# Transposes on two row halves, dt transposes behind slot 5, and a new order of the end, in a fused Mamba and feed-forward layer

## The reference, cut to what matters

```
# layer 1: a mixing of the tokens by condition, then a state space layer
h     = mixed tokens of x                       # [64, 32, 512]
proj  = h @ in_proj_w.T                         # gate 4096, x/B/C 6144, dt 64
xBC   = silu(causal conv of 4 taps over time of proj's x, B, C)
dt_p  = softplus(dt + dt_bias);  A = -exp(A_log)
state = state * exp(dt_p * A) + dt_p * x * B    # for each of 64 heads, 32 steps
y     = state . C + x * D
out   = (y * rsqrt(mean square of its group) * norm_weight * silu(gate)) @ out_proj_w.T
x     = x + out
# layer 2: grouped conv of 9 taps + context, then a dense layer with a selection
v     = conv(x) + c @ c_weight.T + bias
dots  = softmax(v @ centroids.T / 0.1);  hits = dots > 0.01
dense = v @ weight.T + bias
x     = x + where(any hit in this row & cluster of this column was hit, dense, 0)
```

## Time and profile before

| | us |
|---|---|
| median of 3 runs | 1626.84 (1625.94 to 1626.89) |
| the profiled execution's own time | 1627.06 |
| its span | 1625.3 |
| PE busy | 1604.8 (99%) |
| DVE busy | 1059.1 (65%) |
| ACT busy | 845.9 (52%) |
| POOL busy | 773.4 (48%) |

### The profile page before, as it was taken

How to read it: one execution, slowest core, us unless ns; L and a number is a source line. 1 busy time by engine, 2 the same in 40 slices (tenths; PEclk the granted TensorE clock), 3 DMA queues, 4 the chain that set the end, 5 groups by cost and what they waited for, 6 DMA issues and landing times. The chain is left out here.

```text
span 1625.3 us, 31516 instructions
## 1 busy us (share of the span) xinstructions
PE 1604.8 (99%) x12495; PEld 1299.1 (80%) x12495; DVE 1059.1 (65%) x1741; ACT 845.9 (52%) x1372; POOL 773.4 (48%) x731
## 2 busy tenths in 40 slices
PE   9999999999999999999999999999999999999997
PEld 6778888888888888887787888888888888887665
DVE  6876666565656576676686656565667656565455
ACT  4654546555555545565554555555555556544321
POOL 3564644545453645454255554646364545534203
PEclk9999999999999999999999999999999999999999
DMA  5111102011111101011112201111110201116772
GB/s 190 59 53 33 41 20 66 27 53 40 40 53 34 59 16 58 21 53 40 33 41 73 65 28 53 41 40 53 34 59 8 66 21 53 41 36 153 181 156 104
DMA packets 50290, 93.08 MB, mean 57 GB/s; under 512 B 5664, under 2 KB 6304, under 8 KB 50144
## 3 DMA queue, kind: packets, MB, share of 16 engines
q1 hardware_dynamic: 50144, 91.06, 19.6%
HBM read 82.59 MB, written 8.45 MB: 56 GB/s over the span
## 5 line engine op out<-in xcount | busy, mean ns | idle before, releaser
L487 PE MATMUL PS<-xh,wh 128*128 128x512 f32 x1280 | 518.7, 405 | 0.6 <-DVE xl L369 0.6
L487 PE MATMUL PS<-xh,wl 128*128 128x512 f32 x1280 | 500.0, 391 | 0.0
L487 PE MATMUL PS<-xl,wh 128*128 128x512 f32 x1280 | 499.8, 390 | 0.0
L522 DVE SCALAR_TENSOR_TENSOR cb<-PS,P,cb 128x496 f32<-128x496 f32 (+2 forms) x576 | 412.6, 716 | 132.5 <-ACT cb L508 119.0
L184 POOL TENSOR_TENSOR wl<-rw,wh 128x512 fp32r<-128x512 f32 x160 | 211.8, 1328 | 188.6 <-ACT wh L179 170.6
L721 POOL TENSOR_TENSOR ysum<-yq 128x256 f32<-128x256 f32 x128 | 109.4, 855 | 364.0 <-ACT yq L706 363.8
L487 PEld LDWEIGHTS PS<-xh,wl 128*128 128x128 f32 x1280 | 240.2, 188 | 52.9
L487 PEld LDWEIGHTS PS<-xh,wh 128*128 128x128 f32 x1280 | 240.5, 188 | 49.1 <-ACT wh L179 1.0
L487 PEld LDWEIGHTS PS<-xl,wh 128*128 128x128 f32 x1280 | 241.0, 188 | 44.3
L508 ACT ACTIVATE cb<-PS,P 128x512 f32<-128x512 f32 x192 | 148.4, 773 | 205.2 <-PE PS L487 205.2
L650 DVE TENSOR_TENSOR big<-Lt,gmt 128x512 f32<-128x512 f32 x128 | 102.6, 843 | 158.0 <-ACT Lt L588 158.0
(11 more groups left out here) (197 smaller groups left out, 2230.6 us busy)
## 6 DMA issues: line engine op xcount, KB each, us to landing
rw<-in_w_in SPq DMA_DIRECT2D x160, 256.0 KB, 2.7
ro<-in_w_out SPq DMA_DIRECT2D x64, 256.0 KB, 2.9
wh<-x2s SPq DMA_DIRECT2D x32, 258.5 KB, 5.2
wl<-x2s SPq DMA_DIRECT2D x32, 258.5 KB, 5.1
x2s<-acc SPq DMA_DIRECT2D x16, 260.0 KB, 5.5
out_x<-acc SPq DMA_DIRECT2D x16, 256.0 KB, 2.3
acc<-in_x SPq DMA_DIRECT2D x3, 1024.0 KB, 9.4
acc<-in_x SPq DMA_DIRECT2D x4, 256.0 KB, 4.8
```

What stands on the lines that cost most here:

```text
L487: fn = lambda e, k=k, w=w, v=v, i=i: e.matmul(PS[:, bank, :], w[:, m, 128 * k:128 * k + 128], v[:, k, a:a + 512], start=(i == 0), stop=(i ...
L522: dve.op(lambda e, d=d, w=w: e.scalar_tensor_tensor(out=cv[:, :, d:32], in0=pv[:, :, 0:32 - d], scalar=w, in1=cv[:, :, d:32], op0=ALU.mult ...
```

## The change

`A` makes its transposes on two halves of 64 rows each, half `v` into bank `TB[r][v]`; it has two calls instead of four, and its waits are drawn together. Bank numbers are permuted. The dt transposes of stages 1, 16 and 17 go behind slot 5, with another pace of the chain. In layer 2 `ffn_ops` is cut in two (`ffn_rest`), and the order of the last three tiles is interleaved; late tiles get their bias by a matmul of 64 rows (`bias_rows` prepares the operand), ACT scales them by the row selection (`scaled`), and only tile 0 is done on POOL apart.

```diff
-        PP, PT, PG, PY, PO = (0, 1, 4), 2, 3, (5, 6), (7, 7, 5, 6)
-        SEG = (7, 6)
-        TB = (PT, PO[2], PT, PO[0])
+        PP, PT, PG, PY, PO = (0, 1, 2), 6, 3, (4, 5), (7, 7, 5, 4)
+        SEG = (7, 4)
+        TB = ((PO[2], PT), (PT, PO[0]))
...
-        def A(n, i):
...
-            for j in range(4):
-                fn = lambda e, j=j: e.transpose(PS[:, TB[i], 128 * j:128 * j + 128], xs[:, j, a:a + 128], ident)
-                pe.op(fn, "T", (n, i)) if j == 3 else pe.op(fn)
+        def A(n, r):
+            if r == 0:
+                for m in range(6):
+                    pe.wait("silu", (n, m))
...
+                else:
+                    pe.wait("dtx", (n - 1, 3))
+                    pe.wait("acc", (n - 1, 2))
...
+            else:
+                pe.wait("dtx", (n, 1))
                 pe.wait("L", (n, 0))
...
+            for i in (0, 1):
+                a = 128 * (2 * r + i)
+                for j in range(4):
+                    for v in (0, 1):
+                        p, c = slice(64 * v, 64 * v + 64), 256 * i + 64 * j
+                        fn = lambda e, j=j, v=v, a=a, p=p, c=c: e.transpose(PS[:, TB[r][v], c:c + 64], xs[p, j, a:a + 128],
+                                                                         ident[p, 64 * v:64 * v + 64])
+                        pe.op(fn, "T", (n, 2 * r + 1)) if (i, j, v) == (1, 3, 1) else pe.op(fn)
...
-        pace0 = (0, 3, 2, 3, 2, 3, 0, 0, 0, 3)
-        pace = (0, 0, 0, 0, 5, 5, 0, 0, 0, 3)
+        pace0 = (0, 3, 3, 3, 3, 1, 0, 0, 0, 3)
+        pace = (0, 0, 0, 0, 7, 3, 0, 0, 0, 3)
...
+                if n - 1 in block_at and m == 5:
+                    assert not chain
+                    DT_pe(block_at[n - 1], [("acc", (n - 1, 1))])
+                    DT_split(block_at[n - 1])
                 if m == 7:
                     A(n, 0)
-                    A(n, 1)
...
                 if m == 9:
-                    A(n, 2)
-                    A(n, 3)
+                    A(n, 1)
...
-        LATE, APART = 10, 2
+        LATE, APART = 10, 1
...
             q = 0
+            if c == 0 and T >= LATE:
+                pe.wait("br", 3)
+                pe.op(lambda e: e.matmul(PS[:, bank, 0:288], onr, hrow, start=True, stop=False))
...
+        def scaled(T, c):
+            a, b = ((0, 288), (288, 512))[c]
+            act.wait("q", T)
+            act.wait(*(("dn", (T, 1)) if c else ("ff", (T, 0))))
+            src = spots[T][:, a:b] if c else PS[:, ffn_bank(T, 0), 0:288]
+            act.op(lambda e: e.mul(spots[T][:, a:b], src, qs[:, T:T + 1]), "sc", (T, c))
...
+                if step == NT:
+                    ffn_rest(NT - 3)
                 ffn_ops(step - 2)
+                if step < NT - 1:
+                    ffn_rest(step - 2)
+                elif step == NT + 1:
+                    ffn_rest(NT - 2)
+                    ffn_rest(NT - 1)
...
         def finish_late(T):
             d = spots[T]
-            dense(T, 0)
             dve.wait("rsel", 0)
-            dve.wait("dn", (T, 0))
-            dve.op(lambda e: e.scalar_tensor_tensor(out=d, in0=d, scalar=qs[:, T:T + 1], in1=rsel, op0=ALU.mult, op1=ALU.mult), "sel", T)
+            dve.wait("sc", (T, 0))
+            dve.wait("sc", (T, 1))
+            dve.op(lambda e: e.tensor_tensor(d, d, rsel, ALU.mult), "sel", T)
...
+        for T in range(LATE, NT):
+            scaled(T, 1)
+        scaled(LATE, 0)
         rows = y[:, 0, :]
         act.wait("rsel2", 0)
         act.wait("yg", (end_n, 3))
         act.op(lambda e: e.copy(rows, PS[:, PT, :]), "rows", 0)
+        for T in range(LATE + 1, NT):
+            scaled(T, 0)
+        finish(1)
         finish(2)
+        finish_apart(0)
         finish(3)
-        finish_apart(0)
-        finish(4)
-        finish(5)
-        finish_apart(1)
         for T in range(LATE, NT):
             finish_late(T)
-            if T < LATE + 4:
-                finish(T - LATE + 6)
+            finish(T - LATE + 4)
```

More of the change, by code:

```diff
@@ L577, in seg @@
                 else:
-                    pe.wait("xl", 5 + r)
+                    pe.wait("xl", 5 + 2 * r)
                 pe.op(lambda e, r=r: e.matmul(PS[:, SEG[r], :], uf[:, :], avh[:, 512 * r:512 * r + 512], start=True, stop=False))
@@ L588, in expo @@
                 act.op(lambda e, r=r: e.activation(Lt[:, 512 * r:512 * r + 512], PS[:, SEG[r], :], ACT.Exp), "L", (n, r))
-        def A(n, i):
[L591 to L594, removed]
+        def A(n, r):
+            if r == 0:
+                for m in range(6):
+                    pe.wait("silu", (n, m))
                 if n == 0:
                     pe.wait("dre", (0, 1))
-                elif n in block_at:
-                    pe.wait("xl", 4 * block_at[n] + 3)
[L599 to L606, removed]
+                    pe.wait("xl", 7)
+                else:
+                    pe.wait("dtx", (n - 1, 3))
+                    pe.wait("acc", (n - 1, 2))
+                if n in block_at and n >= 1:
+                    pe.wait("xl", 4 * block_at[n] + 3)
             else:
+                pe.wait("dtx", (n, 1))
                 pe.wait("L", (n, 0))
-            for j in range(4):
-                fn = lambda e, j=j: e.transpose(PS[:, TB[i], 128 * j:128 * j + 128], xs[:, j, a:a + 128], ident)
-                pe.op(fn, "T", (n, i)) if j == 3 else pe.op(fn)
+                if n in block_at:
+                    pe.wait("dre", (block_at[n], 1))
+            for i in (0, 1):
[6 more added lines that the diff above has]
+                        pe.op(fn, "T", (n, 2 * r + 1)) if (i, j, v) == (1, 3, 1) else pe.op(fn)
         def G_all(n):
@@ L636, in A_dve @@
             z, r = 4 * n + i, i % 2
-            dve.wait("T", (n, i))
+            b0 = TB[i // 2][0]
+            dve.wait("T", (n, i | 1))
             dve.wait("dtt", 2 * half + tb)
@@ L641, in A_dve @@
             dve.op(lambda e: e.tensor_tensor(
-                dtx[:, r, :].rearrange("p (h c) -> p h c", h=8), PS[:, TB[i], :].rearrange("p (h c) -> p h c", h=8),
-                bc(dtt[:, 4 * tb + i, 8 * g:8 * g + 8].rearrange("p (h o) -> p h o", o=1), 128, 8, 64), ALU.mult), "dtx", (n, i))
+                dtx[:, r, :].rearrange("p (j v c) -> p j v c", j=4, v=2),
+                PS[:, b0:b0 + 2, 256 * r:256 * r + 256].rearrange("p v (j c) -> p j v c", j=4),
+                bc(dtt[:, 4 * tb + i, 8 * g:8 * g + 8].rearrange("p (j v o) -> p j v o", j=4, v=2), 128, 4, 2, 64), ALU.mult), "dtx", (n, i))
         def M_dve(n, i):
@@ L868, in stage @@
                     G_mask(n)
-                turned_now = n == 0 or n - 1 in block_at
-                if m == 6 and not turned_now:
+                if n >= 1 and m == 6:
                     av(n)
@@ L889, in stage @@
                 evac(n, m)
-                if m == 6 and turned_now:
-                    t = block_at[n - 1] if n else 0
+                if n == 0 and m == 6:
                     assert not chain
-                    DT_pe(t, [("acc", (n - 1, 1)) if n else ("xl", 5)])
-                    DT_split(t)
-                    av(n)
+                    DT_pe(0, [("xl", 5)])
+                    DT_split(0)
+                    av(0)
                 if n == 0 and m < 6:
@@ L943, in stage @@
                     if b is not None:
-                        D_pe(b, [("dtx", (n, 0))])
+                        D_pe(b, [("dtx", (n, 1))])
                         chain.extend(D_chain(b))
                 if m == 9:
-                    A(n, 2)
-                    A(n, 3)
+                    A(n, 1)
                     Y(n, 0)
@@ L1115, in ffn, with bias_rows @@
                         PS[:, bank, 0:288], x3_slot(v, T)[:, 128 * k:128 * k + 128],
-                        w[:, k, 288 * c:288 * c + 288], start=(q == 0), stop=(q == 11))
+                        w[:, k, 288 * c:288 * c + 288], start=(q == 0 and not (c == 0 and T >= LATE)), stop=(q == 11))
                     pe.op(fn, "ff", (T, c)) if q == 11 else pe.op(fn)
                     q += 1
+        hrow, lrow = (t[:, :, :].rearrange("p a c -> p (a c)")[0:64, 0:288] for t in (ah, al))
+        def bias_rows():
+            dve.wait("ld_bf", 0)
+            dve.wait("avh", end_n)
+            dve.wait("avl", end_n)
+            dve.op(lambda e: e.tensor_copy(hrow, bB[0:64, 0:288]), "br", 0)
+            dve.wait("br", 0)
+            dve.op(lambda e: e.tensor_tensor(lrow, bB[0:64, 0:288], f(hrow), ALU.subtract), "br", 1)
+            dve.wait("br", 1)
+            dve.op(lambda e: e.tensor_scalar(lrow, f(lrow), C[0:64, C_ID + 32:C_ID + 33], None, ALU.mult), "br", 2)
+            dve.wait("br", 2)
+            dve.op(lambda e: e.scalar_tensor_tensor(out=hrow, in0=f(hrow), scalar=C[0:64, C_ID:C_ID + 1], in1=f(lrow),
+                                                    op0=ALU.mult, op1=ALU.add), "br", 3)
+        def scaled(T, c):
[4 more added lines that the diff above has]
+            act.op(lambda e: e.mul(spots[T][:, a:b], src, qs[:, T:T + 1]), "sc", (T, c))
```

(9 more changed lines are left out.)

## The result

The changed kernel takes 1631.33 us (median of 11 runs, 1627.1 to 1633.34) against 1626.84 us before (11 runs beside them, 1625.88 to 1629.11). The ratio is 1.0026, 95% interval 1.0018 to 1.0033: 0.26% slower, 3.5 us above the forecast of 1627.8 and inside its range. The profiled execution took 1631.01 us with a span of 1629.2.

A forecast was written before the change was run, and what follows sets the result against it. TensorE (busy 99%) was taken as the bound, DVE and POOL at the end. Terms -2.8 (`A`) +2.5 (dt transposes) +1.3 (end) = +1.0 against the profiled 1627.06, 0.2 above the median, gave 1627.8 us, range 1620 to 1634.

The forecast's parts named there:

- The dt transposes, +2.5 in the sum: Move behind slot 5: stage 1 +1.5, stage 17 +1.2, stage 16 0; taken as +2.5 us, bounds -3.8 to +3.3.
- PE, in order, stands from 102.5 to 105.9: 3.3 us: Stage 1, ahead of the dt transposes: TensorE waits 3.3 us for DVE's chain, with slots 6 to 9 behind it.
- The row halves, -2.8: Transposes in `A`: -1.6 over 26 stages, -1.0 in four stages, -0.2 for the first half in three: -2.8 us.
- First half: 1.28 forecast: Transposes between slots 7 and 8: block with its edges 1.28 us instead of 1.34, gain 0.06 a stage.
- Second half 0 in the others: Slot 9, in front of `Y`: gain 0 where `Y` waits for `M` on DVE; 0.26 real in stages 0, 15, 16, last.
- The new wait costs nothing either: Second half of `A`: waiting for the first exponential ahead of the block costs 0, ending 0.1 us before `Y` may start.
- First rival: Transposes in `A`: weight load bounds them, a pair takes 0.112 us, +14, kernel 1644 us; chance 0.15.
- Second (operand ready, 1621.8): Dt transposes find their operand ready, both stalls go: -3.5 instead of +2.5, kernel 1621.8 us; chance 0.12.
- Third (cheaper shape change, 1620): Transposes in `A`: change between full and 64x128 shape is cheaper, 26 x -0.3 more, kernel 1620; chance 0.08.
- +4 to +6, 1632: Stalls behind slot 5 above 3.3 us, or the low clock longer in the tail: +4 to +6, 1632; chance 0.10.
- The end, +1.3: Tail: late tiles 2.10 us each on PE, low clock adding 1.7: +1.3 us; -0.4 with no fall of the clock.
- wait of 0.82 for `x3l`: Tail: ffn(15,1)'s 0.82 us wait behind tile 13's softmax goes; rows come about 0.4 earlier, bounds 0 and 0.82.

The follow-up runs named there:

- e1: Changed kernel with the dt transposes of stages 1, 16 and 17 back behind slot 6, with the old pace: 1625.53 us, ratio 0.9991.
- e12: Changed kernel plus eight unused 512-column products ahead of the dt transposes, in stages 1 and 17 only: 1627.80 us, ratio 1.0005.
- e4: Kernel before with only the transposes on row halves and the bank numbers they need: 1625.12 us, ratio 0.9988.
- e5: e1 with ScalarE's exponential put ahead of the weight split in slot 8: 1615.65 us, ratio 0.9926.
- e6: Kernel before with only ScalarE's exponential put ahead of the weight split in slot 8: 1621.80 us, ratio 0.9968.
- e7: e1 with full transposes in the second half of `A`, keeping one wait ahead of all eight: 1632.67 us, ratio 1.0032.
- e8: e1 with the late tiles' bias product on all 128 rows: 1623.63 us, ratio 0.9982.
- e2: Kernel before with only the dt transposes moved behind slot 5 and the new pace: 1632.53 us, ratio 1.0038.
- e9: e1 with full transposes in the second half of `A`, exponential's wait only before the fourth tile, VectorE waiting per tile: 1625.43 us, ratio 0.9998.

## Why the prediction came out as it did

The direction and the places were right, and one term of the sum was mis-sized: it gave +1.0 us where +4.5 came. That the median lies within 1620 to 1634 is owed to the width of the range, and part by part the errors add up: the row halves gave 1.1 less than the sum had, the dt transposes cost 3.3 more. (Measured one by one the three parts make +5.5; the 1.0 between that and +4.5 lies within the noise and has no other explanation here.)

The dt transposes, +2.5 in the sum, cost 5.8 (e1 against the changed kernel). The step that failed is "PE, in order, stands from 102.5 to 105.9: 3.3 us". The stand was right: 3.21 us idle in stage 1 and 3.20 in stage 17; no wait ahead of `seg` in either any more; and +2.3 for it alone (e12 against e1). What the step left out is the clock behind such a stand, 1.7 us a time. The sum for the end did take a low clock behind a stretch with little for PE; the same row should have been asked of the stand that I forecast myself. Then 3.4 more gives 1631.2. One run of the changed kernel took 1627.1 with a mean clock of 0.999, which leaves room for one low stretch only, as my sum had it; it has no trace, so where that stretch lay is not shown.

The row halves, -2.8, measured -1.7, with an interval of -3.4 to -0.7. First half: 1.28 forecast, 1.29 measured; the gain 0.045 a stage and not 0.06. Stages 15 and 16 gained 0.28 and 0.27 (e4), where 0.3 was forecast; stages 1 and 17, which that sum leaves out, gained 0.16 and 0.18. Second half 0 in the others, and `Y` bound by `M`: right, e5 and e6 show it. "The new wait costs nothing either" held, but without the 0.1 us to spare that the sum had: the block ends where the first `M` does, since it began 0.12 behind the start of `M` (not 0.01) and took 0.64 (not 0.62). e7 shows what the wait costs with a block 0.35 longer: 0.2 a stage.

The Trainium skill ("TensorEngine Tiling (Array Packing)", Key Properties) says that a change of tiling mode drains the engine, without a price. The trace agrees: 0.32 instead of 0.23 to get in, and e8 gives the price of one way in and out with the loads laid bare, 0.4 us. No run separates a drain from the loads.

First rival (weight load bound, 1644): wrong; 16 transposes take 0.64 from the first start to the next shape, where it needs 0.99, and a load of a row half is 138 ns beside 140. Second (operand ready, 1621.8): wrong, the wait is there, and the chain's first steps took 1.26 to 1.39 us again, from 92.81 to 96.88 us, while POOL worked on products of its own from 92.58 to 96.74; whether the one slows the other was not tried. Third (cheaper shape change, 1620): wrong, the edges are those of `X` and `Y`. The smaller case "+4 to +6, 1632", with 0.10, has the time that came but neither of its two conditions: the stands were 3.2, and the low clock in the tail was as long as before. It was the low clock at the dt transposes.

The end, +1.3, measured +1.5 alone (not clear of noise; +1.4 from last `Y` to the end in its trace), with 2.11 for a tile against 2.10, POOL waiting for `sel`, and the low clock of 3.41 us as forecast. Of the wait of 0.82 for `x3l`, said to go, 0.32 stayed.

## What to carry to other kernels

A stall of TensorE of some 3 us is to be priced twice: the stall, and the stretch at 1.2 GHz that can come with it (here 1.7 us each). When a block gets faster in front of a wait, look at what else ends there first; here moving one exponential ahead made the same row halves worth 0.24 us a stage instead of 0.045. When waits are merged, the work that ran ahead of the later one is the price, and it is nothing only as long as that work is short.

## What the runs showed of the hardware

The granted clock fell around a stand of 3.2 us in stages 1 and 17 of the changed kernel and of e2, and did not where eight products filled 2.0 us of the same 3.5 (e12). It did not fall behind the wait of 1.05 us ahead of `seg` in the kernel before. How far from the stand the slow products lie differs: the fall comes 1.35 and 1.38 us after PE has begun again in the changed kernel, 0.1 us after it in e2's stage 1, and in e2's stage 17 while PE still stands.

Other places fit, but not as a rule. In stage 0 the traces of e2, e4 and e7 have stands of 3.2 to 3.4 us in front of `G`, each with a fall; e5 has a fall with one of 1.46, e12 none with one of 1.74. The row and the window of e4:

```profile
37.50 0.66 PE L624 MATMUL PS<-big 128*32 128x32 f32 x32 [3.37 <-ACT big L542]
...
36.56:43.38 6.82, 5.88 (x44) 4.35 (x44) 6.68 (x13) 2.29 (x4) 4.65 (x3) 0.50 0.31 112
```

In the tail, with much the same work on PE around the selection products, eleven of the fourteen traces have a fall and those of e6, e9 and e12 have none; it lasts 3.4 us in seven of them and 6.8 in four. Between executions of one kernel it varies too: for the changed kernel mean clocks of 0.993 to 0.999 go with 1633.34 to 1627.1 us. What decides it is open.
